# Written-out loops, sums loaded two groups behind rows, and GpSimd's splits in another order, in a cross attention with a mixture of experts

## The reference

```python
def attn(query, key, value, ...):          # 16 heads of 16, softmax over the heads of one token
    attn = softmax(einsum('bnhd,bngd->bnhg', q, k) * SCALE)
    x = transpose(einsum('bnhg,bngd->bnhd', attn, v), (0, 2, 1, 3)).reshape(B, N, C)
    return x @ Wp.T + bp

def ffn(x, gate_w, w1, w2, sfc1, sfc2, sfc3):
    shared = (silu(x @ sfc1.T) * (x @ sfc2.T)) @ sfc3.T
    top_w, top_idx = top_k(x @ gate_w.T, 2)              # 2 of 16 experts per token
    dispatch = scatter(softmax(top_w), top_idx)
    h = silu(einsum('td,ehd->teh', xf, w1))
    return shared + einsum('teh,te,edh->td', h, dispatch, w2)

x = x + attn(layernorm(x), ctx, ctx, ...)
x = x + ffn(layernorm(x), ...)
```

## Time and profile before

| | us |
|---|---|
| median of 3 runs (1860.51 to 1875.49) | 1864.77 |
| the profiled execution | 1852.7 |
| its span | 1850.9 |

### The profile page before, as it was taken

How to read it: one execution, slowest core, us unless ns; L and a number is a source line. 1 busy time by engine, 2 the same in 40 slices (tenths; PEclk the granted TensorE clock), 3 DMA queues, 4 the chain that set the end, 5 groups by cost and what they waited for, 6 DMA issues and landing times.

```text
span 1850.9 us, 50328 instructions
## 1 busy us (share of the span) xinstructions
PE 1504.5 (81%) x17109; PEld 1318.8 (71%) x17110; DVE 1345.4 (73%) x3378; ACT 726.3 (39%) x1346; POOL 1234.2 (67%) x1109
## 2 busy tenths in 40 slices
PE   5599999999999999999999999875667676666674
PEld 4588787877787878777878788764656665566563
DVE  6588888888888888888888888863445455454453
ACT  3344444454444444544454445331222222222231
POOL 4387777777777777778777877765455554454455
PEclk9799999999999999999999999987788888888887
DMA  8788889878887988789878887747666675666573
GB/s 208 166 186 180 179 201 182 180 169 213 176 177 160 227 176 174 161 221 183 173 173 216 174 175 157 191 176 237 193 208 199 189 209 161 194 203 198 179 209 115
DMA packets 945833, 344.74 MB, mean 186 GB/s; under 512 B 824088, under 2 KB 898730, under 8 KB 940288
## 3 DMA queue, kind: packets, MB, share of 16 engines
q1 hardware_dynamic: 901680, 216.53, 56.9%
q0 software_dynamic: 33600, 92.91, 14.2%
q10 hardware_dynamic: 10512, 34.79, 5.8%
HBM read 200.37 MB, written 148.15 MB: 188 GB/s over the span
## 4 chain that ended last, share of the span: by engine, by line
PE 40%; DVE 18%; issue 16%; SPq 11%; POOL 5%; DMA 5%; ACT 4%; another core or an unknown queue 1%; DVEq 0%; POOLq 0%; ACTq 0%
SPq L337 4%; SPq L331 4%; PE bank_y L1145 3%; ACT xn L613 3%; PE bank_a L1158 3%; PE bank_y L1143 3%; PE bank_y L1144 3%; PE bank_a L1143 3%; DVE ln_stats L897 2%; PE bank_z L1143 2%; DVE ctx_lo L880 2%; PE bank_a L1297 2%; PE bank_a L1145 2%; PE bank_a L1144 2%; PE bank_u L1143 2%
## 5 line engine op out<-in xcount | busy, mean ns | idle before, releaser
L400 POOL DMA_INDIRECT slots<-xn,slot_i x256 | 281.6, 1100 | 96.0 <-issue 55.7
L517 POOL DMA_INDIRECT sums<-v_area,tail x144 | 144.0, 1000 | 144.4 <-DVE v_area L1096 98.8
L517 POOL DMA_INDIRECT out<-v_area,tail x144 | 143.6, 997 | 135.6 <-DVE v_area L1096 91.6
L1386 PE MATMUL bank_a<-ident,k_area 128*128 128x128 f32 x576 | 96.1, 321 | 140.8 <-DMA k_area<-slots 140.3
L1386 PEld LDWEIGHTS bank_a<-ident,k_area 128*128 128x128 f32 x576 | 77.8, 165 | 150.7 <-DMA k_area<-slots 150.1
L1096 DVE SCALAR_TENSOR_TENSOR v_area<-bank_y,tail,v_area 128x256 f32<-128x256 f32 x288 | 121.4, 478 | 68.4 <-remote 31.2
L690 ACT ACTIVATE th<-bank_z 128x512 f32<-128x512 f32 x72 | 43.0, 597 | 280.9 <-remote 135.6
L1075 DVE TENSOR_TENSOR xn_lo<-v_area,xn_hi 128x512 fp32r<-128x512 f32 x72 | 50.2, 698 | 140.2 <-ACT xn_hi L697 71.4
L409 POOL DMA_INDIRECT sums<-v_area,slot_i x128 | 128.1, 1001 | 33.2 <-issue 29.4
L1143 PE MATMUL bank_y<-wsh_out_hi,hid_hi 128*128 128x256 f32 x512 | 143.1, 279 | 1.3 <-POOL hid_lo L431 1.3
L1144 PE MATMUL bank_y<-wsh_out_lo,hid_hi 128*128 128x256 f32 x512 | 142.8, 279 | 0.0
(11 more groups left out here) (222 smaller groups left out, 5283.9 us busy)
## 6 DMA issues: line engine op xcount, KB each, us to landing
k_area<-slots SPq DMA_DIRECT2D x288, 129.0 KB
v_area<-sums SPq DMA_DIRECT2D x288, 128.0 KB
kv_dram<-w_sb SPq DMA_DIRECT2D x32, 1024.0 KB
x_sb<-in_x_in SPq DMA_DIRECT2D x32, 512.0 KB
ctx_sb<-in_ctx_t SPq DMA_DIRECT2D x32, 512.0 KB
q_dram<-q_sb SPq DMA_DIRECT2D x32, 512.0 KB
k_area<-kv_dram SPq DMA_DIRECT2D x256, 64.0 KB
w_sb<-q_dram SPq DMA_DIRECT2D x256, 64.0 KB
```

The lines of the kernel that those rows point to most:

```text
L400: pool.indirect_dma_start(slots[j], bass.IndirectOffsetOnAxis(ap=slot_i[:, par, j, i:i + 1], axis=0), row_of[j][:, i, :], None).then_inc(S ...
L517: pool.indirect_dma_start(target, bass.IndirectOffsetOnAxis(ap=tail[:, r, t, 1 - j:2 - j].bitcast(u32), axis=0), y_ring[:, r, t, :], None, ...
L1386: last = nc.tensor.transpose(A[t // 2][:, t % 2 * C + k * P:t % 2 * C + (k + 1) * P], x_ring[:, r, t, CHANNEL[j] + k * P:CHANNEL[j] + (k + ...
```

## The change

- In stage 2 the loops of SP, ScalarE, VectorE and GpSimd are written out; register numbers in waits become constants. TensorE's loops stay.
- SP loads the sums of quad n-2 behind the rows of quad n (LAG = 2). The four row registers are no longer shared between rows and sums: `tile_rows` reads the table once for each. Behind the last quads of the first list, the sums of quads 34 and 35 come behind the rows of quads 38 and 39.
- GpSimd, stage 1: `ln1_power(c+1)` stands behind `xn2_split(c-1)`, where `ln1_power(c+2)` stood behind `ln2_power(c)`. Two tiles of base sums, not three, go ahead of `scale_probs`. Of the eight scatters of rows five go ahead of the first two hidden splits, two ahead of the third and one ahead of the fourth.
- ScalarE, stage 1: `turned_out` rounds x of chunk c+2 first, after a wait for TensorE's last matmul that reads the same buffer (`acc_full`), and copies the transposes out behind it.

```diff
-            def load_x(j, n, r, at_rows, first):
+            def load_x(j, n, r, first):
+                rows = tile_rows(x_regs, n)
                 if not first:
                     sp.wait_ge(S["tail_ready"], at(1, n - 4, 1))
...
-            def load_sums(j, n, r, at_rows, first):
+            def load_sums(j, n, r, first):
+                rows = tile_rows(sums_regs, n)
                 if not first:
                     sp.wait_ge(S[f"added{r}"], at(16, n - r, 0))
...
+            LAG = 2
+
+            def load_steps(j, n, new):
+                for r in range(4):
+                    load_x(j, n + r, r, False)
+                    load_sums(j, n + r - LAG, (r - LAG) % 4, new and r < LAG)
...
-            with sp.Fori(4, QUADS - 3, 4) as q:
-                for r in range(4):
-                    at_rows = tile_rows(q + r, r)
-                    load_x(FIRST, q + r, r, at_rows, False)
-                    load_sums(FIRST, q + r, r, at_rows, False)
+            for r in range(4 - LAG):
+                load_sums(FIRST, r, r, True)
+            load_steps(FIRST, 4, True)
+            for q in range(8, QUADS, 4):
+                load_steps(FIRST, q, False)
             sp.wait_ge(S["scattered0"], 16 * BPC * CHUNKS)
-            second_rows = [tile_rows(QUADS + r, r) for r in range(4)]
             for r in range(4):
-                load_x(SECOND, QUADS + r, r, second_rows[r], False)
+                load_x(SECOND, QUADS + r, r, False)
+                if r >= 4 - LAG:
+                    load_sums(FIRST, QUADS + r - 4, r, False)
             for r in range(4):
                 sp.wait_ge(S[f"added{r}"], 16 * QUADS)
...
-            def body(c, par, first, ahead_2):
+            def body(c, par, first, ahead_2, last=False):
                 xn2_split(c - 1)
+                if not last:
+                    ln1_power(c + 1, False)
                 if not first:
-                    scatter_base(c - 2, par, range(3))
+                    scatter_base(c - 2, par, range(2))
                 scale_probs(c)
                 if not first:
-                    scatter_base(c - 2, par, range(3, BPC))
-                scatter(c - 1, 1 - par, SCATTERS[:4])
-                hid_split(c - 1, range(1))
-                scatter(c - 1, 1 - par, SCATTERS[4:5])
-                hid_split(c - 1, range(1, 2))
-                scatter(c - 1, 1 - par, SCATTERS[5:6])
+                    scatter_base(c - 2, par, range(2, BPC))
+                scatter(c - 1, 1 - par, SCATTERS[:5])
+                hid_split(c - 1, range(2))
+                scatter(c - 1, 1 - par, SCATTERS[5:7])
                 hid_split(c - 1, range(2, 3))
-                scatter(c - 1, 1 - par, SCATTERS[6:])
+                scatter(c - 1, 1 - par, SCATTERS[7:])
                 hid_split(c - 1, range(3, SB))
                 ln2_power(c)
                 if ahead_2:
-                    ln1_power(c + 2, False)
                     ctx_split(c + 2)
                     x_split(c + 2)
...
-            def turned_out(c, ahead_2):
+            def turned_out(c, ahead_2, start=False):
+                if ahead_2:
+                    if not start:
+                        act.wait_ge(S["acc_full"], at(2, c, 0))
+                    x_round(c + 2)
                 for k in range(KT):
                     act.wait_ge(S["t2_full"], at(KT, c, k + 1))
                     nc.scalar.activation(xn2_t[:, k, :], XN2T_BANKS[k][:, :], ACT.Copy).then_inc(S["t2_out"], 1)
-                if ahead_2:
-                    x_round(c + 2)
...
-            with act.Fori(4, TOP * QUADS - 7, 4) as q:
-                for r in range(4):
-                    quad(q + r, r, 4, False)
-            for q in range(TOP * QUADS - 4, TOP * QUADS):
+            for q in range(TOP * QUADS):
                 quad(q, q % 4, q, q == TOP * QUADS - 1)
```

## The result

| | us |
|---|---|
| changed kernel, median of 4 runs (1941.04 to 1958.41) | 1947.44 |
| kernel before beside it, median of 4 runs (1852.58 to 1875.49) | 1862.64 |
| ratio, 95% interval | 1.0458 (1.0377 to 1.0538) |
| the profiled execution's span | 1956.6 |

The change made the kernel 85 us slower on the chip on which this pair ran. The forecast was 1857, and 1947 lies beyond its range. The experiments will add a second half to the result: on other chips the same kernel is 6% faster than before.

What follows compares the result with a forecast made beforehand. The prediction took TensorE's own work to bound the attention chunks and SP's issuing to pace the experts' phase, where no engine was full. Terms of +3 there and -11 in the chunks gave -8, so 1857 us; range 1800 to 1895.

Steps and rivals of the forecast that it cites:

- (1): Experts' phase: rows' loads no longer stand behind sums waiting for scatters, so SP's 32.5 us of waits go; -36 us.
- R1: Experts' phase: burstiness of waits, not SP's issuing, makes rows late; TensorE's 125.5 us go; -84, 1770 us; chance 0.12.
- (2): Experts' phase, SP's queue: tile_rows read twice a quad adds register steps 72 times; +30 us, bounds 0 and +103.
- (3): Experts' phase: written-out loops save SP's branches at 16 back-edges and some address work; -3 us.
- R4: Experts' phase: the second read of tile_rows goes at the pace held by scatters; +73, 1930 us; chance 0.05.
- R5: Experts' phase: each of SP's 16 loop back-edges fetched its target, about 4 us; -64, 1793 us; chance 0.03.
- (4): Handover between SP's lists: VectorE stands 6 us, twice, while rows and sums are issued; +12 us, bounds +6 and +20.
- The phase: Experts' phase as a whole, four terms summed: +3 us, bounds -33 and +84.
- (5): Attention chunks: earlier x rounding and moved ln1_power bring xn2_split forward, ending TensorE's wait at shared_z(2); -23 us.
- (6): Attention chunks: copies now wait for x's load, making TensorE's gate late in about half; +12 us, bounds 0 and 50.
- (7): Attention chunks: regrouped scatters and splits leave the split's overlap with VectorE's L880 as today; 0, bounds -33 and +40 us.
- two slower ways: Chunks: back-to-back splits hold VectorE's bias add, 1897 us, chance 0.14; experts' phase: second read held, 1930, chance 0.05.

Runs made afterwards that it cites:

- lag0: Kernel before with loops written out and tile rows read twice, loads in the old order: 1845.6 us on kind H (0.995), 1810.2 on kind F (1.000).
- experts_only: Changed kernel with the whole attention stage as before, only the experts' phase changed: 1724.0 us on kind F (0.953), 1858.9 on kind H (1.001).
- pairs_handover: pairs with SP asking for sums of quads 34 and 35 ahead of rows of quads 38 and 39: 1778.3 us on kind H (0.958).
- changed_2: The changed kernel unaltered, run again beside the kernel before on a chip of kind F: 1696.2 us (0.936).
- group_back_2: Changed kernel with GpSimd's chunk order of scatters and splits as before: 1839.6 us on kind H (0.988); 1700.9 on kind F (0.942).
- group_alone: Kernel before with only GpSimd's new chunk order of scatters and splits: 1786.0 us on kind F (0.989).
- pairs: group_back plus a GpSimd wait for the tanh two quads on, ahead of each quad's third scatter: 1782.7 and 1784.4 us on kind H (0.959, 0.960).
- combined: Changed kernel with base rows 3 and 1, four scatters before two splits, the wait of pairs and the hand-over of pairs_handover: 1650.0 us on kind F (0.913).
- all_eight: Kernel before with base rows 2 and 2, then all eight scatters in a row, then four splits: 1977.0 us on kind H (1.064).

## Why the prediction was wrong

*(1) SP's waits for scatters, -36: the mechanism right, the place wrong.* They are gone in the changed kernel. On kind H TensorE's wait for rows went with them, which R1 had and the forecast had not (125.5 to 5.2 us), but the gain was taken at ScalarE's tanh: the remote waits there rose from 116.4 to 214.2 us in 500. The order of loads cost some 11 us there. On kind F the term came in full and beyond: SP waited 72.1 us in 400 for scatters (`lag0_2`), then 0.5 (`experts_only`), and the order is worth 87 us. That is R1's price of 84, though not its sign, as TensorE's wait for rows stayed at 71.5. The prediction named the holds, took them for holds of the sequencers of SP and ScalarE where TensorE's signal is late, used them for SP's pace alone, and never asked what the new order does to the length of GpSimd's runs.

*(2) The second read, +30, and (3) the loops, -3.* `lag0` has both and took 13 us less than before on kind H (2 to 16) and 0 on kind F. The sum was +27. The second read is hidden (L322 has 144 TENSOR_LOADs of 0.3 us), and R4 falls with it, as does R5, whose 64 us came on neither kind.

*(4) The hand-over, +12.* `pairs_handover` got 6 back on the time and 7.9 on the two quads. VectorE stalls there in the changed kernel, 6.96 and 6.79 us before L1097 at quads 34 and 35 where 6 was forecast (the 7.47 at quad 36 stood before as 7.33), and the mechanism was right; what the order of the two lines costs was half of the term.

The phase was predicted at +3. `experts_only_2` has -2: right as a sum only by luck, since terms were off in both directions.

*(5) and (6), `xn2_split` earlier and x's load at the gate, -23 + 12.* `gap` takes 0.17 us in the median of the changed kernel, and `shared_z(2)` doesn't wait, as predicted. The gate's wait for the copies is put at 0.3 us over the 1040 in `changed_2`, as x's load lands after 4.4, 5.3 and 7.5 us (min, median, max) in the changed kernel and not at 6.2: term (6) was about nothing. `group_back_2` less `experts_only_2` measures -19, where the sum had -11.

*(7) The new order of scatters and splits, counted 0, bounds -33 and +40: this step failed.* It is +108 us on kind H. The working weighed only where a split meets VectorE's ops. That four scatters had become five, and that moving a base row behind `scale_probs` makes a run of seven, was there to be read, and beside it in the earlier trace rows a tanh that started 1.7 us after the end of a run, 8.15 us behind its last matmul. The price from those rows: a tanh that comes due well inside a run starts 1.7 us after its end. In the changed kernel it is 1.4 us after it, and 4.5 us late. The 108 us are shown by putting the order back; that the late signals make them is read from the traces, where in the chunks lateness and loss appear and go together. Of the 3.2 us by which a chunk became longer, 2.8 show as TensorE's longer wait at `o_split`, less 0.8 that it no longer waits at `shared_z(2)`. The rest is TensorE's own work at the lower clock: 926.88 us busy in 1040, or 35.7 in a chunk of 40.0, instead of 34.3 in one of 36.8. The rivals held two slower ways, and neither was this one. On kind F the same step is a gain: -25 us (`group_alone`), which lies within the bounds.

The sentence that the prediction would be wrong above all if SP's pace under scatters weren't a fixed price per step pointed to the right place, the hold, at the wrong engine.

## What to carry to other kernels

When work on one engine is regrouped, count the longest unbroken run of each kind of operation before and after, and ask which engine's wait falls due inside it, and how far in; where the trace of before shows that such runs hold another engine, that price belongs into the sum at every place where a run grows. A wait in the trace that nothing explains is a mechanism to be priced, not a remark. And a tuned order may be right for one chip and wrong for its neighbour: a change worth 6% on one cost 5% on the other, while breaking the runs where the other engine needs it (`pairs`) gained on the one and, within `combined`, did no harm on the other.

## What was not expected of the hardware

- Chips differ in one behaviour. On kind H the updates of TensorE's semaphores and SP's issuing are late while GpSimd's indirect scatters follow one another (a tanh up to 10.8 us behind its matmuls, four loads in 5.83 us); on kind F they are not (0.04 us in `changed_2`'s experts' phase, 1.90 us). The Trainium skill (SBUF — State Buffer, section on two separate sides) says that on the engine side only the port pair shared by VectorE and GpSimd causes contention and that ScalarE never waits for anyone. That agrees with both kinds, as far as the traces go: on kind H the tanh starts 0.02 us behind the late update, so it isn't held at a port. The scatters themselves take the same time on both, one each 1.29 us. The kernel before differs by 50 us (1861 and 1810), the changed one by 252. What makes the updates late stays open.
- The hold sets in inside a run and not at its start. In the experts' phase of the changed kernel 21 tanhs come due in the first 0.8 us of a run of four scatters or more, and none starts over 0.04 us late, though up to 13.9 us of the run were to come. Of the 28 that come due 2.4 us after the start or later, 25 start after the run's end. In the chunk shown the first tanh starts 3.6 us into the run and 0.85 late, and the second, due 1.9 us behind it, after the run's end. `all_eight` has the exception: its second tanh, due 4.8 us into a run of ten, is 1.3 us late in the median.
- A one-element memset between scatters changes nothing (1841 us against 1840); waiting does (1783).
- On kind F the order of SP's loads is worth 87 us, and GpSimd then stands nearly full: in `group_back` 144 scatters stand in one run, and 288 at 1.29 us are 372 of the 443 us from the experts' first tanh to the end.
